# Norms of a set in four column tiles, reciprocals through DRAM, one scaling for a whole set

## The chip, the cores and the metric

One Trainium2 chip, all 8 cores; each core computes one of 8 batch entries, and no data pass between cores. The metric is the device time of the slowest core in microseconds (us).

## The reference

```python
def _l2_normalize_complex(z): return z / sqrt(sum(abs(z)**2, axis=-1, keepdims=True))

q  = (ln(x) @ W_q.T).reshape(B, S, 16, 128)
kv = (ln(x) @ W_kv.T).reshape(B, S, 16, 128)
qf, kvf = _l2_normalize_complex(fft(q)), _l2_normalize_complex(fft(kv))
kvf = cumsum(kvf, axis=1)                      # over the 2048 tokens
values = ifft(qf * kvf).real.reshape(B, S, 2048)
x = x + ln(values @ W_o.T)
x = x + ln(x @ W.T + b + lora(x))              # second half; the change doesn't touch it
```

x is 8 x 2048 x 2048 in float32. The norm that the change is about is the square root of the sum of |z|^2 over the 128 frequencies of one head and one token.

## The kernel before

Each core holds its input transposed in SBUF as XT (128 partitions x 32768 bf16, four blocks of 512 tokens). The 16 heads are taken in pairs. A pair gives two **sets**: set s = 2p holds the key/value spectra (K) of two heads, set 2p + 1 their query spectra (Q). Partitions 0 to 63 are the 64 frequencies of one head and 64 to 127 those of the other; the real and the imaginary part stand side by side, so a set is 128 x 2 x 2048 bf16 (`spec(s)`, lines 375 to 379: KT, QT, or KT2 for set 2).

**Slots.** One set and one block of 512 tokens is a slot: 32 matmuls 128x128 by 512 (`project`, line 352), 16 for the real and 16 for the imaginary part, in two PSUM banks. Slots are numbered i. The first eight alternate between set 0 and 1 block by block (line 341) while the blocks of XT still come in from DRAM, in `NPART` pieces each (line 240); i0 and i1 are the two slots of a block, and i1 runs `lag` parts behind i0 (lines 509 to 554). From slot 8 on (set 2, block 0), slots go set by set (lines 557 to 593). Into a slot's 32 matmuls the code puts `fills` at given matmul numbers: the folds of the next set's weights with the DFT matrix (`fold_w`, in blocks 0 and 1), folds of W_o (`fold_o`, in blocks 2 and 3 up to set 9), the centering of weight rows (`center`: a row sum on ScalarE, two operations on VectorE) and the norm.

**After a slot.** `evacuate` (line 381, ScalarE) copies both PSUM banks to `spec(s)`. `square` (line 392, VectorE) squares and adds the two parts. `norm` (line 401, TensorE) multiplies by a matrix of two 64x64 blocks of ones (BONES): each of the 128 PSUM rows then holds the sum of its head, 64 equal copies each. `invert` (line 409, ScalarE) takes Ln and Exp(-0.5 Ln) of it, and `normalize` (line 418, VectorE) scales the slot. The norm of slot i-1 stands 24 matmuls into slot i, the scaling of slot i-2 at the start of slot i.

**Long pieces.** When all four slots of a set are scaled, `queue_pieces` (line 462) queues two pieces for VectorE: two halves of the running sum for a K set (`scan`, line 428), or two pieces of the complex product Q x K for a Q set (`product`, line 436), which write two of the 16 chunks of VH. `long_piece` takes one after each slot.

**What sets the order.** Every engine's instructions are written out by hand in the order in which the code emits them. Each engine works strictly in that order, and waits are semaphores. Loads of weights and XT are issued on the POOL queue; SP issues constants, stores of folded W_o and later stores. After the last slot the attention output `out_mm` (line 634, 16 matmuls per token tile and quarter, the first 14 of them "early") begins with tile 0 while VectorE still makes the last two chunks of VH (lines 726 to 733). Then the rest of the output and the feed-forward part follow; the change doesn't touch them, except for the order of one group of early matmuls.

Of the kernel before, what the change touches and what calls it, by code (L numbers as in the profile page):

```python
# [101 lines left out]
def build_nc():  # L102
# [20 lines left out]
    wos_d = nc.dram_tensor("wos", [128, 4 * 8192], BF16, kind="Internal")  # L123
    out_d = nc.dram_tensor("out", [S, D], F32, kind="ExternalOutput")
# [20 lines left out]
    SQ2 = [WK[:, 32768 + i * 1536:32768 + i * 1536 + 1024] for i in range(2)]  # L145
    SQS = [WK[:, 33792 + i * 1536:33792 + i * 1536 + 512] for i in range(2)]
    LNT = [WKF[:, 17920 + i * 512:17920 + (i + 1) * 512] for i in range(2)]
    INV = [WK[:, 37888 + i * 512:37888 + (i + 1) * 512] for i in range(2)]
# [48 lines left out]
    def bank(b, lo=0, hi=512):  # L197
        return PS[:, b * 512 + lo:b * 512 + hi]
# [41 lines left out]
    NPART = [8, 8, 8, 8]  # L240
# [221 lines left out]
    def queue_pieces(i):  # L462

        s, b = slots[i]
        if b == 3:
            p = s // 2
            if s % 2 == 0:
                pieces.extend([[(scan, p, 0)], [(scan, p, 1)]])
            else:
                pieces.extend([[(product, p, 0), (product, p, 1)], [(product, p, 2), (product, p, 3)]])  # L470
# [21 lines left out]
    sp.wait(xt_landed[0][-1])  # L492
# [16 lines left out]
    for b in range(4):  # L509
        i0, i1 = 2 * b, 2 * b + 1  # L510
        n = NPART[b]
        lag = 3 if b == 0 else 1
# [5 lines left out]
        for k in range(n):  # L518
            part(i0, k)
            if b == 2 and k < 2:  # L520
                for g in (2 * k, 2 * k + 1):
                    fold_w(("w", 2, 0), g, both(g))
                if k == 1:
# [4 lines left out]
            if b >= 1 and k == 0:  # L528
                norm(i0 - 2)
                invert(i0 - 2)  # L530
                normalize(i0 - 2)
            if k >= lag:
                part(i1, k - lag)
            if b >= 1 and k == n // 2 - 1:
                norm(i1 - 2)
                invert(i1 - 2)
                normalize(i1 - 2)
            if b == 3 and 2 <= k < 4:
                for g in (2 * k - 4, 2 * k - 3):
                    fold_w(("w", 2, 1), g, both(g))  # L540
                if k == 3:
                    raw_load(("w", 3, 1))
                    raw_load(("o", 0, 0))
# [4 lines left out]
        square(i0)
        for k in range(n - lag, n):
            part(i1, k)  # L550
        if b == 3:
            center(("w", 3, 0))
            norm(i0)
            invert(i0)

    whole = [(r, c) for r in range(2) for c in range(NCH)]
    for i, (s, b) in enumerate(slots):
# [9 lines left out]
        if b == 3 and s + 2 < NSET:  # L567
            cent = ("w", s + 2, 0)
# [29 lines left out]
    normalize(last - 1)  # L598
# [6 lines left out]
    for nn in range(4):  # L605
# [3 lines left out]

    l_x = [Landing(nc, "x%d" % i) for i in range(2)]  # L610
# [433 lines left out]
```

How the kernel before makes its waits and increments, by code:

```python
    def wait(self, *tokens):  # L62
        for tok in tokens:
            if tok is None:
                continue
            name, sem, val = tok
            if self.passed.get(name, 0) >= val:
                continue
            self.passed[name] = val
            self.stream.append(lambda e, s=sem, v=val: e.wait_ge(s, v))
# [4 lines left out]
    def mark(self, fn):  # L75
        self.count += 1
        self.stream.append(lambda e: fn(e).then_inc(self.sem, 1))
        return (self.name, self.sem, self.count)
# [17 lines left out]
    def start(self, lane, out, in_):  # L96
        self.count += 16
        lane.do(lambda e: e.dma_start(out, in_).then_inc(self.sem, 16))
        return (self.name, self.sem, self.count)
# [600 lines left out]
    def transpose_xn(t):  # L700
        sp.wait(xn_tok[t])
        dst = VH.rearrange("p (c n) -> p c n", c=16)[:, :, t * 128:(t + 1) * 128]
        land = l_xnt[t % 2]
        land.count += 16
        sp.do(lambda e: e.dma_start_transpose(dst, XN[t % 2]).then_inc(land.sem, 16))
        xnt_ready[t] = (land.name, land.sem, land.count)
```

## Time and profile before

| what | before |
|---|---|
| median of 3 runs | 1007.2 us (1006.26 to 1009.02) |
| the profiled execution, its own time | 1006.4 us |
| its span on the slowest core (core 6) | 1004.7 us |
| spans of the 8 cores | 1001.6 to 1004.7 us |
| granted TensorE clock | 0.996 to 0.998 on all cores |
| VectorE, ScalarE busy | 591.5 us, 340.1 us |

The span runs from the first to the last instruction of the core; the run's time is 1.7 us longer. Engines are PE (TensorE), PEld (its weight loads), DVE (VectorE), ACT (ScalarE), POOL and SP. A line number is that of the kernel before. A recorded matmul lasts longer than the step to the next one, since matmuls are pipelined. A few matmul records are missing.

### The profile page before, as it was taken

How to read it: one execution, taken by the hardware profiler on the slowest of the kernel's cores; microseconds unless marked ns; L12 is line 12 of the kernel's file. 1: busy time of each engine (PE TensorE's matmuls, PEld its weight loads, DVE VectorE, ACT ScalarE, POOL GpSimd, SP SyncE). 2: the span in 40 equal slices, each digit the busy share in tenths (PEclk: the TensorE clock that was granted, in tenths of full speed). 3: DMA queues.
4: the chain of work that ended last, by engine and by line, in shares of the span. 5: the costliest groups of instructions: out<-in, count | busy, mean ns of one | idle time of the engine just before them, and what ended most of it. 6: DMA issues, size and time to landing. Idle time of an engine off the chain costs nothing.

```text
span 1004.7 us, 13984 instructions; the slowest of 8 cores (1001.6 to 1004.7 us)
## 1 busy us (share of the span) xinstructions
PE 970.1 (97%) x4989; PEld 467.9 (47%) x5089; DVE 591.5 (59%) x856; ACT 340.1 (34%) x570; POOL 62.0 (6%) x118
## 2 busy tenths in 40 slices
PE   3989999999999999999999999999999999999996
PEld 2444444444444444444444444444444444444443
DVE  3135755445554466545468777667766656656566
ACT  5145766766667745565330000000000000000001
POOL 8000000000000000000001000000000000000000
PEclk9999999999999999999999999999999999999998
DMA  9997555565566222211089988888696334243232
GB/s 130 158 167 118 85 84 105 105 109 88 86 118 105 64 43 42 43 23 21 1 286 180 172 160 160 146 147 155 132 158 194 96 94 126 64 127 98 91 105 84
DMA packets 67540, 112.23 MB, mean 112 GB/s; under 512 B 37392, under 2 KB 45840, under 8 KB 64912
## 3 DMA queue, kind: packets, MB, share of 16 engines
q0 software_dynamic: 16416, 51.42, 34.6%
q1 hardware_dynamic: 51056, 59.91, 20.6%
q8 instruction: 41, 0.67, 0.3%
q14 instruction: 27, 0.22, 0.1%
HBM read 120.79 MB, written 33.55 MB: 154 GB/s over the span
## 4 chain that ended last, share of the span: by engine, by line
PE 95%; DMA 2%; issue 1%; ACT 0%; POOL 0%; DVE 0%; DVEq 0%; ACTq 0%; POOLq 0%
PE PS L365 43%; PE PS L644 22%; PE PS L831 21%; PE PS L299 3%; DMA XT<-xt 2%; PE PS L783 2%; PE PS L838 1%; PE PS L323 1%; PE PS L404 1%; PE PS L879 0%; POOL WK L98 0%; POOL XT L98 0%; ACT WK L389 0%; ACT XT L911 0%; PE PS L814 0%
## 5 line engine op out<-in xcount | busy, mean ns | idle before, releaser
L365 PE MATMUL PS<-XT,WK 128*128 128x512 bf16 x1999 | 476.9, 379 | 6.0 <-ACT WK L389 2.7
L365 PEld LDWEIGHTS PS<-XT,WK 128*128 128x128 bf16 x2048 | 195.6, 98 | 220.3 <-issue 6.1
L644 PE MATMUL PS<-XT,VH 128*128 128x512 bf16 x1004 | 220.3, 379 | 1.1
L831 PE MATMUL PS<-WK,VH 128*128 128x512 bf16 x808 | 185.6, 379 | 0.6
L644 PEld LDWEIGHTS PS<-XT,VH 128*128 128x128 bf16 x1024 | 100.2, 98 | 120.8
L397 DVE TENSOR_TENSOR WK<-WK 128x1024 bf16<-128x1024 bf16 x60 | 41.5, 692 | 148.3 <-ACT WK L389 147.7
L831 PEld LDWEIGHTS PS<-WK,VH 128*128 128x128 bf16 x819 | 78.9, 98 | 91.0
L656 ACT ACTIVATE SM<-SM 128x1 f32<-128x1 f32 x48 | 14.2, 295 | 260.7 <-DVE SM L692 107.7
L281 ACT ACTIVATE WK<-PS 128x512 bf16<-128x512 f32 x116 | 68.0, 591 | 56.5 <-PE PS L299 55.1
L389 ACT ACTIVATE WK<-PS 128x1024 bf16<-128x1024 f32 x60 | 61.3, 1023 | 32.1 <-PE PS L365 28.5
L847 DVE TENSOR_TENSOR XT<-PS,XT 128x1024 f32<-128x1024 f32 x31 | 37.9, 1223 | 51.8 <-PE PS L814 47.9
L260 ACT ACTIVATE WK<-WK 128x2048 bf16<-128x2048 bf16 x32 | 60.9, 1903 | 14.1 <-DMA WK<-wkv 13.6
L299 PE MATMUL PS<-PHIT,WK 128*128 128x128 bf16 x512 | 49.5, 228 | 15.6 <-DVE WK L264 15.5
L413 ACT ACTIVATE WK<-PS 128x512 f32<-128x512 f32 x64 | 38.2, 597 | 76.5 <-PE PS L404 74.3
L430 DVE TENSOR_TENSOR_SCAN WK<-WK,SM 128x2048 bf16<-128x2048 bf16 x14 | 61.9, 4424 | 1.2
L299 PEld LDWEIGHTS PS<-PHIT,WK 128*128 128x128 bf16 x512 | 40.2, 102 | 42.0 <-issue 16.6
L666 DVE BATCH_NORM_STATS2 SM<-PS 128x6 f32<-128x512 f32 x64 | 41.2, 687 | 29.0 <-PE PS L644 29.0
L262 DVE TENSOR_SCALAR SM<-SM 128x1 f32<-128x1 f32 x32 | 4.9, 154 | 76.8 <-ACT WK L260 76.2
L423 DVE TENSOR_TENSOR WK<-WK 128x1024 bf16<-128x1024 bf16 x60 | 41.1, 685 | 14.3 <-ACT WK L416 14.3
L281 ACT ACTIVATE VH<-PS 128x512 bf16<-128x512 f32 x64 | 37.8, 591 | 33.2 <-PE PS L323 32.3
L831 PE MATMUL PS<-XT,VH 128*128 128x512 bf16 x173 | 47.1, 379 | 0.4
L416 ACT ACTIVATE WK<-WK 128x512 bf16<-128x512 f32 x64 | 40.4, 631 | 8.6
(83 smaller groups left out, 622.9 us busy)
## 6 DMA issues: line engine op xcount, KB each, us to landing
out<-XT SPq DMA_DIRECT2D x15, 1024.0 KB, 5.4
WK<-wkv POOLq DMA_DIRECT2D x16, 512.0 KB, 6.4
WK<-wq POOLq DMA_DIRECT2D x16, 512.0 KB, 6.6
XT<-xt POOLq DMA_DIRECT2D x32, 256.0 KB, 37.5
WK<-wot POOLq DMA_DIRECT2D x16, 512.0 KB, 8.4
wos<-VH SPq DMA_DIRECT2D x32, 256.0 KB, 8.6
XT<-wos SPq DMA_DIRECT2D x4, 2048.0 KB, 9.5
WK<-x POOLq DMA_DIRECT2D x16, 512.0 KB, 8.3
```

The costliest lines, as they stand in the source:

```text
L260: t_sum = act.mark(lambda e: e.activation(RAW[i], RAW[i], AF.Identity, accum_out=SUM[k]))
L281: tok = act.mark(lambda e: e.activation(dst, src, AF.Identity))
L299: return e.matmul(bank(b, k * 128, (k + 1) * 128), RAW[i][:, c * 128:(c + 1) * 128], PHIT[:, :], start=True, stop=True)
L365: return e.matmul(bank(bk + r), WF[s % 3][:, c * 256 + r * 128:c * 256 + (r + 1) * 128], XT[:, b * 8192 + c * 512:b * 8192 + (c + 1) * 512 ...
L389: evac_tok[i] = act.mark(lambda e: e.activation(dst, src, AF.Identity))
L397: dve.do(lambda e: e.tensor_mul(sq.rearrange("p (r t) -> p r t", r=2), src, src))
L416: inv_tok[i] = act.mark(lambda e: e.activation(INV[i % 2], LNT[i % 2], AF.Exp, scale=-0.5))
L423: inv_free[i % 2] = dve.mark(lambda e: e.tensor_mul(t, t, inv))
L430: tok = dve.mark(lambda e: e.tensor_tensor_scan(KC[:, r * 2048:(r + 1) * 2048], spec(2 * p)[:, r * 2048:(r + 1) * 2048], zb, 0.0, ALU.add, ...
L644: return e.matmul(bank(bk), VH[:, c * 2048 + t * 128:c * 2048 + (t + 1) * 128], XT[:, nn * 8192 + c * 512:nn * 8192 + (c + 1) * 512], star ...
L666: dve.do(lambda e, nn=nn: e.bn_stats(ST[:, 6 * nn:6 * nn + 6], bank(ybank(t, nn))))
L831: pe.do(lambda e, c=c: e.matmul(bank(bk), VH[:, c * 2048 + t * 128:c * 2048 + (t + 1) * 128], wchunk(c, nn * 512, (nn + 1) * 512), start=( ...
```

## The change

For sets 0 to 14 the squares of the four slots are gathered side by side (SQS, 128 x 2048), and one group of four matmuls with 32 columns of BONES each (16 from either head) writes the four blocks' sums to the four 32-partition strips of one PSUM bank, by `tile_position`. One Ln and one Exp then do the whole set. SP stores the four strips to DRAM as 32 rows of 2048 tokens (4 KB), and loads each half of these rows back four times, 16 partitions at a time, so that all 128 partitions hold the reciprocals of their head. One product scales the whole set, two slots after its last. The norm of a set stands 14 matmuls into block 0 of the next set. The scaling and the first long piece come in block 2, the second piece in block 3, and the centering that was in block 3 moves to block 2. Set 15 keeps a norm per slot, now 14 matmuls in.

In the first eight slots the lag of block 3 becomes four parts, block 1 of XT comes in 4 pieces instead of 8, folds and the centering move by some parts, and SP starts four constants after the last XT piece. At the end one more group of early output matmuls, (1,1), is moved ahead, and half a scan stands behind the last slot.

```diff
-    NPART = [8, 8, 8, 8]
+    NPART = [8, 4, 8, 8]
     def square(i):
-        dve.wait(evac_tok[i], norm_tok[i % 2])
+        dve.wait(evac_tok[i], norm_tok[own(s)])
...
-        sq_tok[i] = dve.mark(lambda e: e.tensor_add(SQS[i % 2], sq[:, 0:512], sq[:, 512:1024]))
+        sq_tok[i] = dve.mark(lambda e: e.tensor_add(SQS[own(s)][:, b * 512:(b + 1) * 512],
+                                                    SQ2[:, 0:512], SQ2[:, 512:1024]))
+        dve.drain()
+    def norm(s):
+        pe.wait(t_bones, bank_free[7], *[sq_tok[i] for i in last_slots(s)])
+        for b in range(4):
+            def mm(e, b=b):
+                return e.matmul(PS[32 * b:32 * b + 32, 7 * 512:8 * 512], BONES[:, 48:80],
+                                SQS[own(s)][:, b * 512:(b + 1) * 512], start=True, stop=True,
+                                tile_position=(0, 32 * b))
+            if b == 3:
+                norm_tok[own(s)] = pe.mark(mm)
+            else:
+                pe.do(mm)
+    def invert(s):
+        act.wait(norm_tok[own(s)])
+        bank_free[7] = act.mark(lambda e: e.activation(LNT, bank(7), AF.Ln))
         act.drain()
+        act.wait(inv_landed.get(s - 1) if s > 1 else None)
+        inv_tok[s] = act.mark(lambda e: e.activation(INVP[own(s)], LNT, AF.Exp, scale=-0.5))
+        sp.wait(inv_tok[s])
+        rows = inv_d.ap()[s]
+        for b in range(4):
+            t_out = l_inv_out[own(s)].start(sp, rows[:, b * 512:(b + 1) * 512],
+                                            INVP[own(s)][32 * b:32 * b + 32, :])
+        sp.wait(t_out)
+        sp.wait(inv_free[own(s)])
+        for p in range(0, 128, 16):
+            h = 16 * (p // 64)
+            inv_landed[s] = l_inv[own(s)].start(sp, INVB[own(s)][p:p + 16, :], rows[h:h + 16, :])
+    def normalize(s):
+        t = spec(s).rearrange("p (r t) -> p r t", r=2)
+        inv = INVB[own(s)][:, None, :].broadcast_to([128, 2, 2048])
+        dve.wait(inv_landed[s])
+        inv_free[own(s)] = dve.mark(lambda e: e.tensor_mul(t, t, inv))
         dve.drain()
...
-    sp.wait(xt_landed[0][-1])
+    sp.wait(xt_landed[3][-1])
...
-        lag = 3 if b == 0 else 1
+        lag = {0: 3, 3: 4}.get(b, 1)
...
         if b == 3:
-            center(("w", 3, 0))
-            norm(i0)
-            invert(i0)
+            norm(0)
+            invert(0)
...
-        if b == 3 and s + 2 < NSET:
+        if b == 2 and s + 2 < NSET:
             cent = ("w", s + 2, 0)
...
         square(i - 1)
-        fills.append((24, lambda: (norm(i - 1), invert(i - 1))))
-        normalize(i - 2)
-        queue_pieces(i - 2)
+        if b == 0:
+            fills.append((14, lambda: (norm(s - 1), invert(s - 1))))
+        elif s == NSET - 1:
+            fills.append((14, lambda: norm_last(i - 1)))
         project(i, whole, fills)
-        long_piece()
+        if i == 9:
+            normalize(0)
+            queue_pieces(0)
+        if b == 2:
+            normalize(s - 1)
+            queue_pieces(s - 1)
+        if s == NSET - 1 and b >= 2:
+            normalize_last(i - 2)
+        if i + 1 < len(slots):
+            long_piece()
...
-    norm(last)
-    invert(last)
-    normalize(last)
-    queue_pieces(last)
+    norm_last(last)
+    long_piece()
+    normalize_last(last)
+    queue_pieces(NSET - 1)
...
-    for t, nn in ((0, 1), (0, 2), (1, 0), (0, 3)):
+    for t, nn in ((0, 1), (0, 2), (1, 0), (1, 1), (0, 3)):
         out_mm(t, nn, early)
```

`norm_last` and `normalize_last` are the norm, inversion and scaling of one slot as before, for set 15, with the reciprocals in chunk 15 of VH.

## Rows read from the trace of the kernel before

**Rows 1.** The page: busy time by engine, and the chain by engine
```profile
PE 970.1 (97%) x4989; PEld 467.9 (47%) x5089; DVE 591.5 (59%) x856; ACT 340.1 (34%) x570; POOL 62.0 (6%) x118
...
PE 95%; DMA 2%; issue 1%; ACT 0%; POOL 0%; DVE 0%; DVEq 0%; ACTq 0%; POOLq 0%
```

**Rows 2.** Groups by line, TensorE; count, busy us, mean ns, idle before
```profile
L404 PE MATMUL PS<-WK,BONES 128*128 128x512 bf16 x61 | 23.1, 379 | 1.0 <-DVE WK L399 0.9
```

**Rows 3.** Timeline, all engines, a slot with folds; start us, length us, what
```profile
403.60 1.02 ACT L389 ACTIVATE WK<-PS 128x1024 bf16<-128x1024 f32 x1 [0.36 <-PE PS L365]
...
404.20 0.39 PE L299 MATMUL PS<-PHIT,WK 128*128 128x128 bf16 x4
...
404.79 0.69 DVE L397 TENSOR_TENSOR WK<-WK 128x1024 bf16<-128x1024 bf16 x1 [4.18 <-ACT WK L389]
405.56 0.43 DVE L399 TENSOR_TENSOR WK<-WK 128x512 bf16<-128x512 bf16 x1
...
407.13 1.90 ACT L260 ACTIVATE WK<-WK 128x2048 bf16<-128x2048 bf16 x1
...
409.46 0.75 DVE L264 TENSOR_SCALAR WK<-WK,SM 128x2048 bf16<-128x2048 bf16 x1
...
411.61 1.02 ACT L389 ACTIVATE WK<-PS 128x1024 bf16<-128x1024 f32 x1
```

**Rows 4.** Timeline, all engines, a slot without folds
```profile
394.49 7.07 PE L365 MATMUL PS<-XT,WK 128*128 128x512 bf16 x32
...
396.47 1.02 ACT L389 ACTIVATE WK<-PS 128x1024 bf16<-128x1024 f32 x1 [0.36 <-PE PS L365]
...
399.86 0.75 DVE L264 TENSOR_SCALAR WK<-WK,SM 128x2048 bf16<-128x2048 bf16 x1
401.18 0.10 PEld L404 LDWEIGHTS PS<-WK,BONES 128*128 128x128 bf16 x1
401.39 0.38 PE L404 MATMUL PS<-WK,BONES 128*128 128x512 bf16 x1
...
401.61 2.75 PE L365 MATMUL PS<-XT,WK 128*128 128x512 bf16 x12
```

**Rows 5.** Timeline, hand-over from the squares to a norm that waits
```profile
85.77 0.43 DVE L399 TENSOR_TENSOR WK<-WK 128x512 bf16<-128x512 bf16 x1
...
86.45 0.38 PE L404 MATMUL PS<-WK,BONES 128*128 128x512 bf16 x1 [0.95 <-DVE WK L399]
```

**Rows 6.** Timeline, VectorE: a scan half and product pieces with the next operation
```profile
99.95 4.42 DVE L430 TENSOR_TENSOR_SCAN WK<-WK,SM 128x2048 bf16<-128x2048 bf16 x1
104.60 0.69 DVE L397 TENSOR_TENSOR WK<-VH 128x1024 bf16<-128x1024 bf16 x1 [0.23 <-issue]
...
117.55 1.22 DVE L452 TENSOR_TENSOR VH<-WK 128x2048 bf16<-128x2048 bf16 x1
...
121.45 0.69 DVE L397 TENSOR_TENSOR WK<-VH 128x1024 bf16<-128x1024 bf16 x1 [0.23 <-issue]
...
162.12 2.29 DVE L440 TENSOR_TENSOR VH<-WK 128x4096 bf16<-128x4096 bf16 x1
...
165.32 1.23 DVE L449 TENSOR_TENSOR VH<-VH 128x2048 bf16<-128x2048 bf16 x1
```

**Rows 7.** Timeline, TensorE, before slot 8
```profile
54.93 1.02 PE L365 MATMUL PS<-XT,WK 128*128 128x512 bf16 x4 [2.72 <-ACT WK L389]
...
86.76 3.18 PE L365 MATMUL PS<-XT,WK 128*128 128x512 bf16 x14
```

**Rows 8.** The tile XT: issues of its loads, first and last; all issues' time to landing
```profile
L98 POOL DMA_DIRECT2D XT<-xt x32: 535/589/1118, 3.8 to 24.3; - x32
...
DMA to landing us min/median/max: 17.3/37.5/57.0
```

**Rows 9.** DMA issues by line: KB each, median us to landing
```profile
out<-XT SPq DMA_DIRECT2D x2, 128.0 KB, 3.1
```

**Rows 10.** All DMA issues (line 98): ns of one, min/median/max, first and last start
```profile
L98 SPq DMA_DIRECT2D x1s<-WK x16: 320/325/686, 546.0 to 751.6; - x16
```

More of the change, by code:

```diff
@@ L144, in build_nc @@
     KC = WK[:, 28672:32768]
[L145 to L148, printed above, removed]
+    SQ2 = WK[:, 32768:33792]
+    LNT = WKF[:, 17920:18432]
+    SQS = [VH[:, 4 * 2048:5 * 2048], WK[:, 33792:35840]]
+    INVP = [VH[:, 7 * 2048:7 * 2048 + 512], WK[:, 39424:39936]]
+    INVB = [VH[:, 6 * 2048:7 * 2048], WK[:, 37376:39424]]
     T1A = VH[:, 14 * 2048:16 * 2048]
@@ L390, in evacuate, with own @@
         bank_free[bk] = bank_free[bk + 1] = evac_tok[i]
+    def own(s):
+        return 0 if s == 0 else 1
     def square(i):
@@ new lines, in build_nc, with norm_last @@
+    INVL = VH[:, 15 * 2048:16 * 2048]
+    def norm_last(i):
+        b = slots[i][1]
+        pe.wait(sq_tok[i], bank_free[7])
+        norm_tok[1] = pe.mark(lambda e: e.matmul(bank(7), BONES[:, :], SQS[1][:, b * 512:(b + 1) * 512],
+                                                 start=True, stop=True))
+        act.wait(norm_tok[1])
+        bank_free[7] = act.mark(lambda e: e.activation(LNT, bank(7), AF.Ln))
+        act.drain()
+        act.wait(vh_ready[13])
+        inv_tok[i] = act.mark(lambda e: e.activation(INVL[:, b * 512:(b + 1) * 512], LNT, AF.Exp, scale=-0.5))
@@ L460, in build_nc, with queue_pieces @@
     pieces = []
[L462 to L470, printed above, removed]
+    def queue_pieces(s):
+        p = s // 2
+        if s % 2 == 0:
+            pieces.extend([[(scan, p, 0)], [(scan, p, 1)]])
+        else:
+            pieces.extend([[(product, p, 0), (product, p, 1)], [(product, p, 2), (product, p, 3)]])
     def long_piece():
@@ L519, in build_nc @@
             part(i0, k)
-            if b == 2 and k < 2:
-                for g in (2 * k, 2 * k + 1):
+            if b == 2 and 2 <= k < 4:
+                for g in (2 * k - 4, 2 * k - 3):
                     fold_w(("w", 2, 0), g, both(g))
-                if k == 1:
+                if k == 3:
                     raw_load(("w", 3, 0))
@@ L527, in build_nc @@
                     fold_w(first[3], g, both(g))
[L528 to L531, printed above, removed]
             if k >= lag:
                 part(i1, k - lag)
[L534 to L539, printed above, removed]
+            if b == 3 and 5 <= k < 7:
+                for g in (2 * k - 10, 2 * k - 9):
                     fold_w(("w", 2, 1), g, both(g))
-                if k == 3:
+                if k == 6:
                     raw_load(("w", 3, 1))
@@ L597, in build_nc @@
     square(last)
-    normalize(last - 1)
+    normalize_last(last - 1)
     l_wo = [Landing(nc, "wo%d" % i) for i in range(4)]
@@ L604, in build_nc, with wo_load @@
         sp.wait(*pair)
-    for nn in range(4):
+    def wo_load(nn):
         sp.wait(block_last[nn])
@@ L608, in build_nc @@
                                         wos_d.ap()[:, nn * 8192:(nn + 1) * 8192]))
+    for nn in range(4):
+        wo_load(nn)
     l_x = [Landing(nc, "x%d" % i) for i in range(2)]
```

37 lines of the change are left out of this document (17 added, 20 removed).

## The prediction

> **What bounds the kernel now.** I read the page first: TensorE is busy for 97% of the span and the chain that ended last is 95% TensorE [rows 1]. So time is won or lost only where TensorE gets fewer instructions or waits more. The groups by line show what the change can remove: 64 norm matmuls of line 404 (61 of them recorded), and before them 1.0 us of idle in all [rows 2]. The whole trace therefore holds almost no wait for the squares that feed a norm; the present order hides VectorE entirely. Then I read one slot of the projection (one set, one block of 512 tokens) on all engines, because what the change does is to put VectorE's work elsewhere relative to a norm [rows 3]. Below, (s,b) is the slot of set s and block b, and times inside a slot count from its first matmul.
>
> **Prices of a slot.** 32 projection matmuls take 401.39 - 394.49 = 6.90 us, 0.216 each, and the norm matmul between 401.39 and 401.61 another 0.22 [rows 4]. With twelve matmuls from 401.61, four of them in the new slot, the slot of rows 3 begins at 404.20 - 4 x 0.216 = 403.34. Its evacuation starts at 0.26 and ends at 1.28, its squares run from 1.45 to 2.65. From this evacuation to the next it is 411.61 - 403.60 = 8.01 us with four folds and a norm [rows 3]; 7.79 without the norm; a slot without folds is 6.90, so a fold costs (7.79 - 6.90) / 4 = 0.22. ScalarE's row sum of a centering starts at 3.79 (after two fold evacuations), and VectorE's second centering step ends at 409.46 + 0.75 - 403.34 = 6.87. Without folds the same step ends 399.86 + 0.75 - 396.47 = 4.14 after the evacuation began, at 4.40. A square of a slot costs VectorE 0.69 + 0.08 + 0.43 = 1.20, now plus a drain of 0.08. From its end to the matmul that waits for it: 86.45 - (85.77 + 0.43) = 0.25 [rows 5]. A 128x4096 bf16 product takes 2.29 [rows 6]; the scaling of a whole set has that size and type, so 2.29 + 0.08 = 2.37. First half of a scan 4.42 (no drain behind it), second half 104.60 - 99.95 = 4.65, first product piece 165.32 + 1.23 - 162.12 + 0.08 = 4.51, second 121.45 - 117.55 = 3.90 [rows 6].
>
> **Term 1, norm matmuls.** From slot (2,0) on, 57 of the 64 norms lie on the path (slots 7 to 63); four full ones stay for set 15. 53 x 0.216 = 11.4 us go. The seven earlier ones belong to the start (term 3). Fourteen groups of four 32-column matmuls come (sets 1 to 14). No row shows a column tile. The near end is 0.22, if four share one pass; the far end is four passes with their weight loads of 0.10 in the open and TensorE's pipe emptied once, 4 x 0.32 + 0.16 = 1.4, the 0.10 is from [rows 4], and 0.16 is 379 - 216 ns, how long a recorded matmul outlasts its step [rows 2]. I take one pass with the pipe emptied on both sides, 0.22 + 2 x 0.16 = 0.54; where TensorE waits in front anyway, the first emptying is free, 0.38. Twelve groups wait (term 2): 12 x 0.38 + 2 x 0.54 = 5.6 us. The Trainium skill (TensorEngine Tiling, Key Properties) says that changing the tiling mode drains TensorE, and (TensorE: Matmul & The Clock Gate, Part 3) that three column tiles gave 2.38x. By the drain rule the group costs what I take; without it the gain would be 14 x 0.22 = 3.1 instead of 5.6. No row here shows either.
>
> **Term 2, the squares become late.** This decides. The norm of a set is now 14 matmuls into (s+1,0), not 24, and needs the square of (s,3). The scaling and the first long piece (scan or product) are queued on VectorE in (s+1,2), the second in (s+1,3). VectorE works in order, so in (s,2) it holds: the squares of (s,1), the centering for set s+2 (moved here from block 3), the scaling of set s-1, the first piece; in (s,3) the squares of (s,2) and the second piece; and only then the squares of (s,3). For s = 3, 5, 7, 9 (a scan, slots with folds), from the start of (s,2): centering done 6.87, scaling 9.24, first half 13.66, squares 1.28 more 14.94, second half 19.59, squares 20.79, TensorE released 21.04. TensorE comes to the norm at 2 x 7.79 + 14 x 0.216 + 2 x 0.22 = 19.04. Wait 2.0. For s = 4, 6, 8 (a product): 9.24 + 4.51 + 1.28 + 3.90 + 1.45 = 20.38, wait 1.3. For s = 10 to 13 blocks 2 and 3 have no folds: centering done 4.40, TensorE at 13.80 + 3.46 = 17.26; a scan (11, 13) gives 4.40 + 2.37 + 4.42 + 1.28 + 4.65 + 1.45 = 18.57, wait 1.3; a product (10, 12) 17.91, wait 0.6. Set 14 has no centering; its squares come at 16.72, wanted at 16.8: none. Set 2 carries one piece more (scaling of set 0 and the first half in (2,1), the second half and the first product piece in (2,2) and (2,3)): 6.87 + 2.37 + 4.65 + 1.28 + 4.51 + 1.45 = 21.13 against 19.04, wait 2.1. Set 15, slot by slot: in (15,2) VectorE holds squares to 2.73, scaling of 14 to 5.10, one slot's scaling to 5.87, half a scan to 10.29, squares and hand-over 11.74; the norm is wanted in (15,3) at 7.12 + 3.02 = 10.14, wait 1.6. Sum: 4 x 2.0 + 3 x 1.3 + 2 x 1.3 + 2 x 0.6 + 2.1 + 1.6 = 19.4 us. What waits behind: the Ln and Exp of the set and the centering for the next slot's fold on ScalarE; with the norm at 5.4 the centering ends on VectorE at about 10.5, the fold wants it at about 10.9. No further loss, but little room.
>
> **Term 3, the start.** Before slot (2,0) TensorE idles 2.72 us up to 54.93 and 0.95 up to 86.45 [rows 5, 7], and seven norms go from there too. I cost all of that at nothing, since the tokens' transfers hide it: the last XT piece is issued at 24.3 and the longest takes 57.0 us to land, so 81.3 [rows 8]; the same bytes go first in the new order. With the lag of four in block 3, six parts of four matmuls remain after the last part of slot (0,3) can start: 81.3 + 24 x 0.216 = 86.5, then the first norm group 0.54: slot (2,0) begins at 87.0, now at 86.76 [rows 7]. +0.3. Two more moves cost nothing by the same cover: the load of raw weights (3,0) is issued two parts later but lies behind the XT pieces in its queue anyway; SP starts the constants PSI, SGN, IDENT and GB only when the last XT piece is there, at 81, while the first fold that wants PSI is in (2,2), at about 105. Ln and Exp of set 0 now stand before the evacuation of (1,3): it ends near 89.8, the squares near 91.1, the norm of set 1 is wanted at 90.5: +0.8.
>
> **Term 4, through DRAM.** SP issues 4 stores and 8 loads per set; a 128 KB store takes 3.1 us to land [rows 9], an issue costs SP 0.33 [rows 10]. Inversion 1.9, then 4 x 0.33 + 3.1 + 8 x 0.33 + 3.1 = 10.2, together 12 us; nothing else is queued behind on SP but store_o. The norm is at 3.5 to 5.4 in (s+1,0), so the rows are there at 16 to 18; the scaling wants them in (s+1,2) at 20 or later, for set 14 at 17. I cost it at nothing. The cover is two slots. Ends: nothing, or 5 us, if 256 more small transfers meet the weight loads, first in sets 0 and 1, whose rows share the queue with the end of the XT loads. ScalarE loses 45 Ln and 45 Exp; it bounds nothing, so nothing.
>
> **Term 5, the end.** After the last slot VectorE has squares to 2.73, a slot's scaling 3.5, half a scan 8.2, the last scaling 8.9, products 13.4 and 17.3. The six early groups of 14 matmuls last 84 x 0.216 + 0.22 = 18.4. No wait, by 1 us. Without the sixth group ((1,1) is moved up) it would be 2 us.
>
> **Sum.** -11.4 + 5.6 + 19.4 + 0.3 + 0.8 = +14.7. The profiled execution took 1006.4 us (span 1004.7), 0.8 below the median of the runs shown: 1006.4 + 14.7 = 1021.1 us. A difference under about 0.3% (3 us) can't be told from none.
>
> **The rivals.** (a) As summed, 1021 us: 0.50. (b) The column tiles don't overlap: a group of 0.86 to 1.4 instead of 0.4 adds 6 to 14 us, 1027 to 1035. For it: the four matmuls have distinct weights and nothing in this trace shows two matmuls in one step. 0.14. (c) Faster: VectorE is in time. The point is the wait per set: below (11.4 - 5.6)/14 = 0.4 us each the removed matmuls win. It would take a chain from centering to last square shorter by 1.5 us, for instance a scaling of 128x4096 that runs at twice the pace of the product, or a centering that ScalarE starts earlier than in the slot of rows 3. Then only the start's 0.3 stays: 1006.4 - 11.4 + 5.6 + 0.3 = 1001 us, and 998 with groups of 0.22. Against it: 13 us of VectorE work from rows stand in a stretch of 12.2 us. 0.17. (d) The rows from DRAM come late and VectorE stands at the scaling, with all that is queued behind it. The point is 20 to 24 us into (s+1,0), where the scaling wants them; each microsecond over it is one more of wait in each of the 13 sets that wait: one over gives 1034. Against it: 4 us of cover. 0.10. (e) A third of the waits walked, 6 us, cancels against the norms: 1006.4 - 11.4 + 5.6 + 1.1 + 6 = 1008, between 1004 and 1011. 0.09.
>
> **Numbers.** The likeliest is (a), 1021.1; its own range is 1014 to 1029 (0.4 us of error per wait on 13 waits gives 5, the price of a group 2.5 more). For 8 in 10 the range takes in (b) and half of (d) above, and (e) below: 1004 to 1032. Faster by over 0.3%: (c) and a little of (e), 0.20. Within 0.3%: 0.08. Slower: 0.72.
>
> **What would show it.** Right: L404's successor shows TensorE idle before the first matmul of a group, released by VectorE's second square, near 2.0 us in odd sets 3 to 9, 1.3 in even, 0.6 to 1.3 in 10 to 13, none for 14, and 1.6 once in set 15; total idle by that releaser 15 to 20 us. The step from the first matmul of a group to the next projection shows the group's price. Slot (2,0) begins near 87 us. Slots of blocks 1 to 3 last 7.8 and 6.9 us, 0.22 less than now. VectorE is never released by the landing of the rows except in sets 0 and 1. Wrong: if that idle is under 5 us, term 2 has failed; if slot (2,0) begins before 84, the start was not held by its transfers; if VectorE's scaling waits for DMA in the middle of the run, it is rival (d).

## The result, and the profile after

The changed kernel takes 1027.2 us (median of 5 runs, 1026.26 to 1028.18), the one before 1007.2 in 5 runs: ratio 1.0197, 95% interval 1.0185 to 1.0209. That is 20 us slower, where 14.7 were forecast and the range ended at 1032. The profiled execution took 1027.2 us, its slowest core (core 5) 1025.6. Five cores have spans of 1023.4 to 1025.6 us at a granted clock of 0.991 to 0.993, three (2, 4 and 7) 1017.3 to 1018.2 at 0.995; before, all lay between 1001.6 and 1004.7. Which cores are the short ones changes from run to run. In some executions of any of these kernels a group of cores shows a lower granted clock throughout; times so disturbed are left out below, which leaves experiment 10 without a time.

The page of after, to be read against [rows 1]:

```profile
PE 972.8 (95%) x5089; PEld 463.2 (45%) x5089; DVE 588.0 (57%) x811; ACT 289.4 (28%) x480; POOL 58.9 (6%) x114
...
PE 68%; DVE 11%; DMA 7%; DVEq 7%; ACT 3%; issue 2%; SPq 1%; POOL 1%; ACTq 0%; another core or an unknown queue 0%; POOLq 0%
```

TensorE was 95% of the chain and is 68% now; VectorE and DMA have come in. From the waits of core 5 (engine, line, releaser; us in all, times, longest):

```profile
PE PS L418 <- DVE WK L405: 23.3, 13, 11.8
...
PE PS L303 <- DVE WK L268: 16.9, 3, 13.0
...
DVE WK L477 <- DMA VH<-invs: 8.0, 1, 8.0
...
DVE WK L477 <- DMA WK<-invs: 4.9, 1, 4.9
...
PE PS L457 <- DVE WK L405: 1.4, 1, 1.4
```

L418 is the norm group, L405 the second square, L477 the scaling of a set, L457 the norm of a slot of set 15. L303 is a fold that waits for centered weights, L268, at the start of the kernel; before, the same wait was 16.1 us on core 5 and 15.5 on core 6, so it is no part of the difference. Where [rows 2] had 1.0 us of idle before all norms, TensorE now stands 23.3 us before thirteen of the fourteen groups of sets 1 to 14; half of it, 11.8, is one wait, in set 2.

**An ordinary set.** VectorE, and TensorE around the group, in the timeline of core 5 for (3,2), (3,3) and the start of (4,0):

```profile
219.80 0.75 DVE L268 TENSOR_SCALAR WK<-WK,SM 128x2048 bf16<-128x2048 bf16 x1
220.47 2.29 DVE L477 TENSOR_TENSOR WK<-WK 128x4096 bf16<-128x4096 bf16 x1
...
222.84 4.42 DVE L484 TENSOR_TENSOR_SCAN WK<-WK,SM 128x2048 bf16<-128x2048 bf16 x1
...
227.18 0.67 DVE L403 TENSOR_TENSOR WK<-WK 128x1024 bf16<-128x1024 bf16 x1
...
228.44 4.42 DVE L484 TENSOR_TENSOR_SCAN WK<-WK,SM 128x2048 bf16<-128x2048 bf16 x1
...
233.03 0.69 DVE L403 TENSOR_TENSOR WK<-WK 128x1024 bf16<-128x1024 bf16 x1 [0.16 <-issue]
233.79 0.43 DVE L405 TENSOR_TENSOR WK<-WK 128x512 bf16<-128x512 bf16 x1
...
234.36 0.40 PE L418 MATMUL PS<-WK,BONES 128*32 128x512 bf16 x4 [1.50 <-DVE WK L405]
234.69 1.47 PE L369 MATMUL PS<-XT,WK 128*128 128x512 bf16 x6
```

From the centering to the last square VectorE has no gap over 0.2 us, as term 2 walked it, and TensorE stands 1.50 us plus the 0.16 by which a recorded matmul outlasts its step: 1.66, forecast 2.0. The group costs 0.33 from its first matmul to the next projection.

**Set 2.** The transfers of sets 0 and 1 on core 5, then what VectorE and TensorE make of them (POOL's wot and wkv are raw weights of 512 KB each):

```profile
81.02 1.06 POOL L98 DMA_DIRECT2D WK<-wot  x2
...
86.95 2.07 SPq L98 DMA_DIRECT2D invs<-VH  x4
...
96.06 4.70 SPq L98 DMA_DIRECT2D VH<-invs  x8
...
100.86 2.69 SPq L98 DMA_DIRECT2D invs<-WK  x4
...
101.78 0.53 POOL L98 DMA_DIRECT2D WK<-wkv  x1 [7.05 <-PE PS L303]
...
104.76 2.29 DVE L477 TENSOR_TENSOR WK<-WK,VH 128x4096 bf16<-128x4096 bf16 x1 [7.98 <-DMA VH<-invs]
...
108.89 4.90 SPq L98 DMA_DIRECT2D WK<-invs  x8
...
118.66 2.29 DVE L477 TENSOR_TENSOR WK<-WK 128x4096 bf16<-128x4096 bf16 x1 [4.86 <-DMA WK<-invs]
...
132.91 0.62 PE L418 MATMUL PS<-WK,BONES 128*32 128x512 bf16 x4 [11.80 <-DVE WK L405]
```

The stores of set 0 go out from 87 on, and SP can issue the loads only at 96, when the stores have landed. VectorE stands at the scaling twice, 8.0 and 4.9 us, and everything behind it in its order is late: the squares that end the list come at 132.8. Core 2, one of the three short ones, has its stores of set 1 issued from 97.8 on, ahead of POOL's weight load at 100.45, so its rows are asked for at 102.0; its wait before set 2's group is 4.6. In core 5 the stores meet the load and the rows are asked for 6.9 us later. The idle before this group sorts the cores: 4.2 to 4.6 on cores 2, 4 and 7, 10.3 to 12.4 on the others.

**The clock after it.** Windows of core 5 (us, PE busy, PEld, DVE, ACT, POOL, PEclk, DMA share, GB/s):

```profile
120.00:132.00 12.00, 1.11 (x9) 0.42 (x6) 11.20 (x8) 0.60 (x1) 0.00 (x0) 0.66 0.42 84
133.00:137.00 4.00, 4.00 (x16) 1.63 (x16) 0.00 (x1) 3.23 (x5) 0.00 (x0) 0.50 0.08 19
137.00:141.00 4.00, 4.00 (x25) 1.96 (x23) 3.83 (x5) 1.63 (x3) 0.53 (x1) 0.93 0.22 45
```

After 11.8 us without a matmul TensorE works at the level of 1.2 GHz (0.50) from 132.9 to 137, which loses half of 4.1 us, and in the next 4 us 0.07 of them: 2.3 us.

### The profile page after: what moved, and what is told of

The parts are those of the page before. It is cut to its first block, busy times and chain, and to the rows that moved or that the text cites. A ratio compares the mean times of both kernels' runs of the same rounds, so it can differ in the third digit from the quotient of the medians.

```text
span 1025.6 us, 13976 instructions; the slowest of 8 cores (1017.3 to 1025.6 us)
## 1 busy us (share of the span) xinstructions
PE 972.8 (95%) x5089; PEld 463.2 (45%) x5089; DVE 588.0 (57%) x811; ACT 289.4 (28%) x480; POOL 58.9 (6%) x114
## 4 chain that ended last, share of the span: by engine, by line
PE 68%; DVE 11%; DMA 7%; DVEq 7%; ACT 3%; issue 2%; SPq 1%; POOL 1%; ACTq 0%; another core or an unknown queue 0%; POOLq 0%
PE PS L704 22%; PE PS L891 21%; PE PS L369 19%; DVEq L81 7%; DMA XT<-xt 5%; DVE WK L484 4%; ACT WK L264 2%; PE PS L303 2%; PE PS L843 1%; DVE VH L494 1%; PE PS L898 1%; DVE WK L403 1%; SPq L98 1%; DVE WK L405 1%; DMA WK<-wkv 1%
## 5 line engine op out<-in xcount | busy, mean ns | idle before, releaser
L704 PE MATMUL PS<-XT,VH 128*128 128x512 bf16 x1024 | 221.3, 379 | 0.0
L704 PEld LDWEIGHTS PS<-XT,VH 128*128 128x128 bf16 x1024 | 100.2, 98 | 120.7
L403 DVE TENSOR_TENSOR WK<-WK 128x1024 bf16<-128x1024 bf16 x60 | 41.4, 689 | 145.7 <-ACT WK L393 141.7
L303 PE MATMUL PS<-PHIT,WK 128*128 128x128 bf16 x512 | 49.9, 229 | 17.0 <-DVE WK L268 16.9
L303 PEld LDWEIGHTS PS<-PHIT,WK 128*128 128x128 bf16 x512 | 40.5, 103 | 44.1 <-issue 18.9
L891 PE MATMUL PS<-XT,VH 128*128 128x512 bf16 x189 | 50.6, 379 | 0.0
L915 DVE BATCH_NORM_STATS2 SM<-XT 128x6 f32<-128x512 f32 (+1 forms) x64 | 40.0, 668 | 2.8
L738 DVE SCALAR_TENSOR_TENSOR WK<-PS,SM,WK 128x1024 bf16<-128x1024 f32 x32 | 39.6, 1279 | 1.4
L750 DVE BATCH_NORM_STATS2 SM<-WK 128x6 f32<-128x512 bf16 x64 | 39.6, 681 | 1.5
## 6 DMA issues: line engine op xcount, KB each, us to landing
XT<-wos SPq DMA_DIRECT2D x4, 2048.0 KB, 11.1
```

Of the source, the lines that this page charges most:

```text
L303: return e.matmul(bank(b, k * 128, (k + 1) * 128), RAW[i][:, c * 128:(c + 1) * 128], PHIT[:, :], start=True, stop=True)
L403: dve.do(lambda e: e.tensor_mul(SQ2.rearrange("p (r t) -> p r t", r=2), src, src))
L704: return e.matmul(bank(bk), VH[:, c * 2048 + t * 128:c * 2048 + (t + 1) * 128], XT[:, nn * 8192 + c * 512:nn * 8192 + (c + 1) * 512], star ...
L891: pe.do(lambda e, c=c: e.matmul(bank(bk), VH[:, c * 2048 + t * 128:c * 2048 + (t + 1) * 128], wchunk(c, nn * 512, (nn + 1) * 512), start=( ...
L915: dve.do(lambda e, k=k, ch=ch: e.bn_stats(st[:, 6 * ch:6 * ch + 6], y[:, k * w:(k + 1) * w]))
```

## The experiments

The first four runs ask what each part of the 20 us is. All ratios are to the kernel before.

**1. Norms 24 matmuls in.** The late squares should cost nothing if TensorE asks for them 10 matmuls later.

```diff
-            fills.append((14, lambda: (norm(s - 1), invert(s - 1))))
+            fills.append((24, lambda: (norm(s - 1), invert(s - 1))))
-            fills.append((14, lambda: norm_last(i - 1)))
+            fills.append((24, lambda: norm_last(i - 1)))
```

> The changed kernel with the norm group of a set, and the norms of set 15, 24 matmuls into the next slot instead of 14. Theory (VectorE's squares are late by a fixed amount): TensorE comes 10 matmuls and a fold, 2.4 us, later; the waits of sets 3 to 13 (0.2 to 1.5 us of idle each, 11.0 in all) and of set 15 (1.4) go to zero, that of set 2 falls by 2.4, so 15 us less than the changed kernel: 1012 us. Rival (the backlog of VectorE only moves and is met by the next wait): the idle of TensorE stays above 15 us and the time above 1022. The rows from DRAM are asked for 2.4 us later; if they have no cover, VectorE waits for them in the middle sets.

Measured: 1017.5 us, ratio 1.0092 (1.0073 to 1.0110), 10 us less than the change and not the 15 expected. Spans by core 998.6 to 1013.9. From the waits of core 3:

```profile
DVE WK L477 <- DMA WK<-invs: 15.3, 7, 5.8
...
PE PS L418 <- DVE WK L405: 10.8, 3, 9.2
...
PE PS L704 <- DMA XT<-wos: 3.1, 1, 3.1
```

Of the 10.8 us, 9.2 are set 2's. So most of the waits of the ordinary sets are gone (1.6 us are left on this core), which settles term 2 as their cause; but VectorE now waits for rows in ordinary sets too, which it did not with the norm at 14, and the first loads of folded W_o (L704) come late at the output. Between 200 and 520 us a store took 1.6 us to land in the change (median, core 5) and takes 4.0 here (core 0); the loads of the rows went the other way, from 4.7 to 2.4.

**2. Four full matmuls in place of four column tiles.** All four write the same bank, so what stays there are block 3's sums.

```diff
-                return e.matmul(PS[32 * b:32 * b + 32, 7 * 512:8 * 512], BONES[:, 48:80],
+                return e.matmul(bank(7), BONES[:, :],
                                 SQS[own(s)][:, b * 512:(b + 1) * 512], start=True, stop=True,
-                                tile_position=(0, 32 * b))
```

> The changed kernel with the four 32-column matmuls of a group replaced by four full 128-column ones into the same bank (left out: the right sums for blocks 0 to 2; the factors of the scaling are those of block 3 only, in other rows). Theory (four column tiles share one pass, group 0.33 us from the first to the next projection): the group takes 4 x 0.216 = 0.86, 15 groups, +7 to +8 us: 1035. Rival (tiles don't overlap or switching modes costs as much): within 2 us of the changed kernel, 1025 to 1029.

Measured: 1034.2 us, ratio 1.0264 (1.0248 to 1.0280), 7 us more than the change. A group in its timeline:

```profile
203.09 1.02 PE L418 MATMUL PS<-WK,BONES 128*128 128x512 bf16 x4 [1.02 <-DVE WK L405]
203.95 1.46 PE L369 MATMUL PS<-XT,WK 128*128 128x512 bf16 x6
```

0.86 us to the next projection against 0.33: 0.53 more for each of 15 groups is 8.0 us, and 7 were measured. The column tiles share one pass; rival (b) is out.

**3. Sets 0 and 1 without the wait for the rows.** Their scaling multiplies by the array of squares, which is there already.

```diff
-        inv = INVB[own(s)][:, None, :].broadcast_to([128, 2, 2048])
-        dve.wait(inv_landed[s])
+        inv = (SQS if s < 2 else INVB)[own(s)][:, None, :].broadcast_to([128, 2, 2048])
+        dve.wait(inv_landed[s] if s >= 2 else None)
```

> The changed kernel, but the scaling of sets 0 and 1 takes the squares as factor and doesn't wait for the rows (left out: right factors for sets 0 and 1; all stores, loads and VectorE work stay). Theory (the long wait of set 2, 4 to 12 us by core, comes from the late rows of sets 0 and 1): that wait falls to the 1.8 us that VectorE's own work makes, TensorE keeps its clock, 10 to 11 us less: 1016, and the spans of the cores within 2 us of each other. Rival (VectorE or DMA work of set 2 itself): no change.

Measured: 1014.7 us, ratio 1.0075 (1.0058 to 1.0092). All cores lie at 1011.6 to 1013.1, at a clock of 0.996 to 0.998. After the start, one wait of the changed kernel's list is left at size:

```profile
PE PS L418 <- DVE WK L405: 12.9, 13, 1.8
```

So the late rows of two sets cost 12.5 us of the 20 and the spread between cores. The other 7.5 are what the waits of the ordinary sets cost over what the removed norms save.

**4. W_o's first two loads later in the code.** If these two loads delay the stores of set 0, issuing them after slot (2,0) should help.

```diff
                     raw_load(("w", 3, 1))
-                    raw_load(("o", 0, 0))
-                    raw_load(("o", 1, 0))
...
+        if i == 8:
+            raw_load(("o", 0, 0))
+            raw_load(("o", 1, 0))
```

> The changed kernel with the two first loads of W_o (1 MB of DRAM each) issued after slot (2,0) instead of before it. Theory (the first rows are late because their small transfers share the engines with the end of the POOL queue's loads): the rows of set 0 land 3 us sooner, the wait of set 2 falls by 3 to 8 us: 1020 to 1024. Rival (the round trip takes as long whatever else runs): no change, 1027.

Measured: 1026.9 us, ratio 1.0193 (1.0171 to 1.0215). The edit did not move anything: POOL does not wait for TensorE at this place, and it still issues the two loads at 79.75 us (core 0), ahead of slot (2,0). The order of the code is the order of one engine only.

**5. POOL waits for the stores.** Now with waits (`inv_out` is what `invert` gets from its last store): the two W_o loads behind set 0's stores, the load after (2,1) behind set 1's.

```diff
             norm(0)
             invert(0)
+            pool.wait(inv_out[0])
+            raw_load(("o", 0, 0))
+            raw_load(("o", 1, 0))
...
+        if i == 9:
+            pool.wait(inv_out[1])
```

> The changed kernel, with the POOL queue made to wait for the stores of set 0's rows before it issues the first two loads of W_o, and for the stores of set 1 before it loads raw weights (4,1). Theory (a small store on SP that is still in flight when POOL issues a 1 MB load lands only with that load, 6 to 7 us later; both early sets met one): the loads of set 0's rows start at 89 to 90 instead of 94 to 96, those of set 1 within 2 us of the last store on all cores instead of 5 us on the slow ones; the wait of set 2 falls from 4 to 12 us to 2 to 4 on all cores: 1016 to 1019 us. Rival (the cores differ for another reason, the round trip itself is slow): the wait of set 2 stays above 8 us on the slow cores, 1024 to 1028.

Measured: 1027.5 us, ratio 1.0205 (1.0190 to 1.0219). A miss. Core 4's timeline:

```profile
85.48 1.73 SPq L98 DMA_DIRECT2D invs<-VH  x4
88.41 4.22 SPq L98 DMA_DIRECT2D VH<-invs  x8
88.88 1.06 POOL L98 DMA_DIRECT2D WK<-wot  x2 [9.33 <-DMA invs<-VH]
...
103.31 2.29 DVE L479 TENSOR_TENSOR WK<-WK,VH 128x4096 bf16<-128x4096 bf16 x1 [8.00 <-DMA VH<-invs]
```

The stores of set 0 now land within 1.2 us of the last issue (7.0 on core 5 of the change), so they had been held by loads in flight. But the held loads go out 0.5 us after the first row load, and the rows need until 103.3. The stores of set 1, issued from 92.7 on, now meet the held loads: the rows of set 1 are asked for only at 106.4. The contention moved from the stores of set 0 to its row loads and to the stores of set 1.

**6. The same with the norms 22 in.**

```diff
-            fills.append((14, lambda: (norm(s - 1), invert(s - 1))))
+            fills.append((22, lambda: (norm(s - 1), invert(s - 1))))
```

> The kernel with both gates on POOL and the norms 22 matmuls into the slot instead of 14. If the two causes (order on VectorE; late rows of sets 0 and 1) are separate and are all: no wait before a norm group over 0.5 us, 1000 to 1002 us, 0.6% faster than before. If the rows of set 1 still come late on some cores: 1004 to 1010.

Measured: 1023.0 us, ratio 1.0157 (1.0143 to 1.0172). A miss: cores at 1005.3 to 1021.5, set 2's wait 4.3 us on core 1 and 13.2 on core 3.

**7. And one store in place of four.** The array in DRAM becomes 4 x 32 x 512, so the rows come back in pieces of 1 KB.

```diff
-        for b in range(4):
-            t_out = l_inv_out[own(s)].start(sp, rows[:, b * 512:(b + 1) * 512],
-                                            INVP[own(s)][32 * b:32 * b + 32, :])
+        t_out = l_inv_out[own(s)].start(sp, rows.rearrange("b h t -> (b h) t"), INVP[own(s)])
```

> As with both gates and 22 matmuls, and the four stores of a set made one (rows of 1 KB in DRAM, so the eight loads move 1 KB pieces instead of 4 KB). Theory (what the round trip costs is SP's issuing and the wait for the store, not the size of the pieces): the loads start 1.5 us sooner, the time is the same within 1 us of the kernel with four stores where nothing waits, or up to 3 us less where set 2 still waits. Rival (1 KB pieces are slow): landing of the rows takes 2 us or more longer and VectorE waits in more sets.

Measured: 1015.4 us, ratio 1.0092 (1.0072 to 1.0111), and from the waits of core 5:

```profile
PE PS L418 <- DVE WK L405: 18.3, 1, 18.3
...
DVE WK L479 <- DMA VH<-invs: 10.8, 1, 10.8
DVE WK L479 <- DMA WK<-invs: 10.5, 1, 10.5
```

Two things are told apart here. In the ordinary sets nothing waits any more, neither VectorE for rows nor TensorE for squares. All that is left is sets 0 and 1, worse than ever on this core. One store is no cure by itself: that of set 1 went out at 92.99, behind POOL's load at 92.87 and the two held ones, and its rows were asked for only at 106.5.

**8. Centering back in block 3.** The change without that one move, norms 14 in.

```diff
-        if b == 2 and s + 2 < NSET:
+        if b == 3 and s + 2 < NSET:
             cent = ("w", s + 2, 0)
```

> The changed kernel with the centering for set s+2 back in block 3 (norms at 14 matmuls). By the walk of the prediction it then holds up the second piece instead of the scaling: sets 3 to 9 wait as before (idle 1.5 and 1.0 us), sets 10 to 13 (0.2 to 1.0 us of idle) wait no more: 2 us less, 1025. Rival (moving the centering to block 2 was what made the squares late): the idle of sets 3 to 9 goes too, 8 us more: 1017.

Measured: 1021.9 us, ratio 1.0157 (1.0141 to 1.0173), 4 to 5 us less than the change. Core 3 waits 1.29 us before the groups of odd sets (1.50 in the change) and 0.55 before even ones (1.03); its long wait turned up at a fold:

```profile
127.56 0.58 PE L303 MATMUL PS<-PHIT,WK 128*128 128x128 bf16 x4 [9.79 <-DVE WK L268]
133.19 0.41 PE L418 MATMUL PS<-WK,BONES 128*32 128x512 bf16 x4 [0.36 <-DVE WK L405]
```

The move of the centering is a part of the ordinary waits, 0.2 to 0.5 us of a set in sets 3 to 8, not their cause; by the walk of term 2, the two pieces and the scaling behind one another are the rest.

**9. Sets 0 and 1 slot by slot.** Their norm, inversion and scaling as in the kernel before, without the trip through DRAM; groups from set 2 on, 22 matmuls in. The core of the edit:

```diff
+            if b >= 1 and k == 0:
+                norm_slot(i0 - 2)
+                invert_slot(i0 - 2)
+                normalize_slot(i0 - 2)
...
-        if b == 0:
-            fills.append((14, lambda: (norm(s - 1), invert(s - 1))))
+        if i == 8:
+            fills.append((24, lambda: (norm_slot(7), invert_slot(7))))
+        if i <= 9:
+            normalize_slot(i - 2)
+            queue_pieces(s - 2 + i - 8)
+        if b == 0 and s > 2:
+            fills.append((22, lambda: (norm(s - 1), invert(s - 1))))
```

> Sets 0 and 1 scaled slot by slot, as in the kernel before and with no DRAM trip; groups of column tiles, rows through DRAM and whole-set scaling from set 2 on; norms 22 matmuls in. If the order on VectorE and the late rows of sets 0 and 1 are all that costs: no wait before a norm over 0.5 us, the start as before; against the kernel before 52 full norms of 0.216 go and 13 groups of 0.43 come, -5.6 us: 1001 to 1002. Rival (the whole-set scheme has a further cost, such as rows late in the middle sets): 1005 or more, with VectorE's waits for rows passed on to TensorE.

Measured: 1008.0 us, ratio 1.0012 (1.0003 to 1.0022): a miss, the rival's figure came. Four cores have spans of 998.2 and 998.3, four 1003.3 to 1006.6. From the waits of core 0 (1005.9):

```profile
DVE WK L501 <- DMA WK<-invs: 14.2, 9, 2.5
PE PS L418 <- DVE WK L405: 5.8, 7, 1.3
PE PS L738 <- DMA XT<-wos: 2.8, 1, 2.8
```

L501 is the scaling, L738 the output. On core 1 (998.2) the first two are 8.0 and 2.3, and the third is not there. By its short cores this order is faster than every core of before (998.2 against 1001.6 to 1004.7); on the others rows that come late in the ordinary sets, 3.5 us more before the groups on core 0 than on core 1, and the late loads at the output take it away.

**10. POOL's loads held until the rows have landed.** The gates of number 5, now on `inv_landed`.

```diff
+            pool.wait(inv_landed[0])
+            raw_load(("o", 0, 0))
+            raw_load(("o", 1, 0))
...
+        if i == 9:
+            pool.wait(inv_landed[1])
```

> The changed kernel with the POOL queue's loads of W_o held until the rows of set 0 have landed (not only their stores), and the load of weights (4,1) until those of set 1 have. Theory (small transfers of SP, stores or loads, wait behind 1 MB loads of POOL that are in flight): the rows of set 0 land within 2 us of their last issue, near 94, VectorE never waits for them; set 1's still meet the held loads and are late, and TensorE may wait for the late W_o. Rival (the rows need over 8 us by themselves): VectorE waits for set 0 as in the changed kernel, 5 to 8 us.

Its time (1045.1 us) is not used; core 1, whose span was 1020.4 us, is read in the timeline:

```profile
85.52 1.72 SPq L98 DMA_DIRECT2D invs<-VH  x4
88.47 3.53 SPq L98 DMA_DIRECT2D VH<-invs  x8
...
95.23 1.06 POOL L98 DMA_DIRECT2D WK<-wot  x2 [15.64 <-DMA VH<-invs]
95.51 2.29 DVE L477 TENSOR_TENSOR WK<-WK,VH 128x4096 bf16<-128x4096 bf16 x1 [0.16 <-issue]
...
103.25 0.38 PE L327 MATMUL PS<-WK,PSI 128*128 128x512 bf16 x1 [1.72 <-DMA WK<-wot]
...
110.98 1.91 ACT L264 ACTIVATE WK<-WK 128x2048 bf16<-128x2048 bf16 x1 [4.73 <-DMA WK<-wkv]
...
128.22 0.62 PE L418 MATMUL PS<-WK,BONES 128*32 128x512 bf16 x4 [6.02 <-DVE WK L405]
```

Without the W_o loads beside them, the rows of set 0 are there 9.7 us after the first store, where experiment 5 needed 17.8, and VectorE does not wait for them, nor for those of set 1. The price stands in the last three rows. TensorE waits 1.72 us for weights that were held. The raw weights behind them land so late that the centering ahead of set 1's scaling can start only at 111, and set 2's group still waits 6.02 us. Holding the large loads moved the wait once more.

**11. Number 9 with the norms 14 in.** The edit is 22 to 14 in both places.

```diff
-            fills.append((22, lambda: (norm(s - 1), invert(s - 1))))
+            fills.append((14, lambda: (norm(s - 1), invert(s - 1))))
```

> The same with the norms of groups and of set 15 at 14 matmuls. Theory (squares late): idle of 1.5, 1.0 us (odd, even sets 3 to 9), 0.2 to 1.0 (10 to 13) and 1.4 (set 15) comes back, 12.4 us, with 0.1 to 0.2 us of emptied pipe each 14 us over the kernel at 22: 1015. Rival (the order matters only together with the late rows): within 3 us of it.

Measured: 1012.3 us, ratio 1.0054 (1.0041 to 1.0068), all cores at 1009.3 to 1010.7. The 12 us over the short cores of number 9 are in the main the waits before groups and norms, term 2 of the forecast, now on every core alike: 10.7 to 11.1 and 1.4 us, against 2.3 and none on core 1 of number 9. At 14 the stores start 2.6 us before POOL's load of that slot (154.8 and 157.3 on core 0), VectorE does not wait for rows, and the cores don't spread.

**12. Number 9 with one store.** Sets 0 and 1 slot by slot, groups 22 in, and the store of number 7.

```diff
-            t_out = l_inv_out[own(s)].start(sp, rows[:, b * 512:(b + 1) * 512],
-                                            INVP[own(s)][32 * b:32 * b + 32, :])
+        t_out = l_inv_out[own(s)].start(sp, rows.rearrange("b h t -> (b h) t"), INVP[own(s)])
```

> The kernel with sets 0 and 1 slot by slot and the norm groups 22 matmuls in, now with the four stores of a set's reciprocals made one (one DRAM array of 4 x 32 x 512, so the rows come back in 1 KB instead of 4 KB pieces). Theory (in the middle sets what is left is the stores and the row loads that meet the 1 MB weight load which POOL issues at the same time; one store goes out 1.0 us earlier than the last of four and ahead of it): VectorE has no wait for rows (12.8 us in 8 waits without this edit), TensorE waits under 1 us before the groups of sets 3 to 14 in place of 2 to 6, and all cores come near 998, so the median at 999 to 1002 us, 0.992 to 0.995 of before. Rival (the spread of the cores comes from the output's loads of folded W_o and not from the rows): VectorE's waits go and the median stays at 1007 to 1008, ratio 1.000. Third (1 KB pieces make the row loads slower than they save): waits for rows stay or grow, 1008 to 1015.

Measured: 1001.6 us (1000.20 to 1002.17 in 5 runs), before 1007.2: ratio 0.9944, interval 0.9929 to 0.9958. It beats both kernels. All cores lie at 994.7 to 998.7, clock 0.997 to 0.998. From its groups by line, core 0 (count, busy us, mean ns, idle before):

```profile
L501 DVE TENSOR_TENSOR WK<-WK 128x4096 bf16<-128x4096 bf16 x12 | 27.4, 2285 | 0.3 <-issue 0.3
...
L418 PE MATMUL PS<-WK,BONES 128*32 128x512 bf16 x52 | 5.2, 390 | 0.0
```

and the transfers of set 2 in its timeline:

```profile
156.56 0.34 SPq L98 DMA_DIRECT2D invs<-WK  x1
157.04 0.53 POOL L98 DMA_DIRECT2D WK<-wkv  x1 [7.71 <-PE PS L303]
158.55 4.17 SPq L98 DMA_DIRECT2D WK<-invs  x8
```

The store is out 0.5 us before POOL's load, the rows are asked for at 158.6; in number 9, where the four stores (from 155.4 to 157.1) straddled POOL's load at 156.0, core 0 asked for them at 163.2. No scaling waits for rows and no group for squares, on any core. The time then agrees with the prices alone: 52 norms of 0.216 go, 11.2 us, and 13 groups of 0.43 come, 5.6; that is -5.6 us, and -5.6 was measured (by the interval -4.2 to -7.2).

## Why the prediction was right, and where it failed

By its own terms, from core 5 of after against the profiled core of before (spans 1025.6 and 1004.7, +20.9):

| term | forecast | measured |
|---|---|---|
| 53 norms removed | -11.4 | -11.4 by the same price, not measured alone |
| 14 groups | +5.6 | +4.7: 13 x 0.33 + 0.43 |
| waits, sets 3 to 13 and 15 | +17.3 | +14.4 |
| wait, set 2 | +2.1 | +12.0, and 2.3 at half clock |
| start and norm of set 1 | +1.1 | -0.8 |
| end | 0 | 0, no idle before L704 |
| sum | +14.7 | +21.2 |

- **Term 1 and the groups.** One pass, as taken. An unwaited group (set 14, first matmul at 517.03, the last projection ahead of it starting at 516.72) costs 0.10 in front and 0.33 behind, 0.43, forecast 0.54; behind a wait 0.33, forecast 0.38. Experiment 12 bears out norms and groups together. (The "gain" of 3.1 in the forecast's term 1 is what fourteen groups would cost; a slip of the word.) The Trainium skill (TensorEngine Tiling, Key Properties) has it that a change of the tiling mode drains TensorE. These rows agree with a small price of that kind: 0.43 is 0.21 more than one matmul's step, and 0.32 had been allowed.
- **Term 2.** Right in place, order and sign. Measured with the 0.16 in each: 1.66 in sets 3, 5, 7 and 9 (2.0 forecast), 1.18 or 1.19 in 4, 6 and 8 (1.3), 0.32, 0.80, 0.31 and 1.16 in 10 to 13 (0.6, 1.3, 0.6, 1.3), 1.6 in set 15 (1.6), none in 14. The walk was up to 0.5 us too long. In the rows of (3,2) to (4,0) above, VectorE takes 14.42 us from the start of the centering step to the end of the last square, where the walk has 14.67, and the group starts 0.14 later, where it has 0.25. The first part is drains charged that VectorE partly hides: the scaling starts at 220.47, before the centering step that began at 219.80 has run its 0.75. Set 2's own part of its wait can be read in experiment 3, where no rows are waited for: 1.84 + 0.16 = 2.0, forecast 2.1. The 16.72 that the walk gives for set 14 adds up to 16.24 from its own prices; neither makes a wait.
- **Term 3.** Slot (2,0) begins at 85.40 on core 5, so 87.0 was 1.6 too late. Over the eight cores it begins at 84.1 to 85.5, before at 84.3 to 86.8, 0.8 us earlier in the mean (core 5: 85.41 before, no gain; core 7: 2.1). The forecast was 0.3 later: the start did gain a little, which term 3 had at nothing. The norm of set 1 waits 0.42 + 0.16, forecast 0.8.
- **Term 4 is the step that failed.** It costed the trip through DRAM at nothing, with 3.1 us for a landing from a store of 128 KB [rows 9] in a quiet stretch. For sets 2 to 14 that holds: VectorE waited for rows only in sets 0 and 1. For those two, whose danger it named without pricing it above 5 us, it is wrong. The stores of set 0 had landed 9 us after their issue began, and the scaling wanted the rows at 96.8 and 113.8 (the starts of the two waits). The rows missed both, and VectorE's order gave the loss on to set 2's squares: 9.9 us over the forecast wait, and 2.3 at the low clock, which the forecast did not have. Experiment 3 prices it at 12.5 us of the median.
- **The rivals.** (b) is refuted by experiment 2. (c) needed a chain shorter by 1.5 us; it was shorter by at most 0.5. (e) needed a third of the waits; 14.4 of 17.3 us came, set 2 apart. (d) was put at the wrong place: its mechanism came, not in the thirteen ordinary sets but in the first two. It did come in ordinary sets once the norm stood at 22 or 24, in numbers 1, 6 and 9.

The errors thus went against each other: 2.9 us too much for the ordinary waits, 1.9 for the start and 0.9 for the groups, and 12.2 us too little for set 2, behind the rows of two sets. With that last error alone the forecast's own sum would have come to 1033 us, outside its range, so that 1027 lies inside is in part luck. The direction is not: term 2 alone, as measured in the ordinary sets, outweighs what the norms save.

## What to carry to other kernels

Batching work per set saves instructions on the bound engine only if the engine that feeds it isn't thereby given its whole list just before the deadline: walk the in-order engine's list from the last fixed point to the release, as term 2 does, and move the consumer, not only the producer. A small transfer on which an engine waits has to be timed against the large ones of the other queues, not priced alone: here four stores begun 2.6 us before the large load let the rows be asked for 3.0 us after the first store (number 11), begun 0.6 us before it 7.8 us after (number 9), and one store 0.5 us before it 2.0 us after (number 12). That one store was worth 6.4 us in the median (number 12 against number 9). The batched form did pay, 0.6%, with the first two sets left slot by slot, the norms 22 matmuls in, and one store for a set.

## What the runs showed of the hardware

- **Small transfers beside large ones.** Landing times of the stores of core 5 in the stretch 76 to 112 us and over the whole run of the change (out<-in, count, KB each, median us to landing):

```profile
invs<-VH SPq DMA_DIRECT2D x4, 32.0 KB, 6.6
...
invs<-WK SPq DMA_DIRECT2D x56, 32.0 KB, 1.6
```

  The same 32 KB store takes 1.6 us as a rule and 6.6 when weight loads of POOL are in flight. The Trainium skill (DMA: Bandwidth & Descriptors, Issuing engines are not separate DMA queues) states that transfers started by different engines run on the same 16 DMA engines and interleave. The traces agree that they share, but in the interleaving the small one came out four times later. By what share each queue is served was not tried.
- **The clock.** 11.8 us without matmuls left TensorE at 0.50 for over 4 us of dense work behind it. That wait cost 2.3 us more than itself. Core 2, whose wait before the same group was 4.64 us, was at 0.50 from 125 to 129 too, so the short cores paid at the clock as well. Where no wait after the start was over 1.8 us (experiment 3) the mean clock was that of the kernel before, 0.996 to 0.998.
- **Column tiles.** Four matmuls of 32 columns, each 402 ns in the records (mean of 56), take 0.33 us together from the first start to the next projection; four of 128 columns into the same bank take 0.86 (experiment 2).
